# Five matmul passes for six in fc1, by weights in units of their first group's scale, and w2 rounded by ScalarE

## What is computed

```python
# layer 1, on n = layernorm(x)
pre = n @ W + b                                  # 256 x 1024
i, f, o, z = split(pre)
i = 10 * tanh((i + input_bias) / 10);  f = -softplus(f);  o = sigmoid(o);  z = tanh(z)
# a scan over time, for each of the 256 channels, with running maximum m
m' = max(f + m, i);  c = exp(f + m - m') * c + exp(i - m') * z
n' = exp(f + m - m') * n + exp(i - m');  h = o * c / (n' + 1e-6)
x = x + h / rms(h) * scale
# layer 2, on g = layernorm(layernorm(x)) * gamma + beta
w1 = (fc1_q - 128) * fc1_scales[row // 128]      # 256 x 1024, two groups of 128 rows
w2 = (fc2_q - 128) * fc2_scales[row // 128]      # 1024 x 256, eight groups
out = x + 0.5 * (silu(g @ w1 + b1) @ w2 + b2)
```

## Time and profile before

| | |
|---|---|
| median of 3 runs | 316.35 us (316.30 to 316.56) |
| the profiled execution | 317.67 us, its span 315.9 us |
| PE busy | 307.7 us |
| DVE busy | 268.2 us |
| ACT busy | 229.2 us |
| POOL busy | 134.0 us |
| DMA | 16.31 MB |

### The profile page before, as it was taken

The page is one execution under the profiler, slowest core; times in us unless marked ns, Lnnn a source line. Parts: engine busy times, 40 slices in busy tenths (PEclk is TensorE's granted clock), DMA queues, the critical chain, the costliest instruction groups (busy, mean ns, idle before and its releaser), DMA issues.

```text
span 315.9 us, 4861 instructions
## 1 busy us (share of the span) xinstructions
PE 307.7 (97%) x1780; PEld 267.0 (85%) x1780; DVE 268.2 (85%) x473; ACT 229.2 (73%) x372; POOL 134.0 (42%) x131
## 2 busy tenths in 40 slices
PE   8999998998999999999999999999999999999996
PEld 6778787886997889988898889988899899899896
DVE  3999969999999999999989997889969998764431
ACT  3598986698699956798776969489684966931930
POOL 2072177300396258214940188012999365153000
PEclk9999999899999999999999999999999999999999
DMA  7990042410000020021000300000000100100101
GB/s 269 362 381 22 0 83 53 100 33 0 2 1 2 33 100 4 0 76 59 1 2 33 100 2 0 33 32 4 3 0 2 66 0 2 66 0 19 50 2 66
DMA packets 11239, 16.31 MB, mean 52 GB/s; under 512 B 720, under 2 KB 10192, under 8 KB 10704
## 3 DMA queue, kind: packets, MB, share of 16 engines
q1 hardware_dynamic: 10512, 13.12, 12.0%
q0 software_dynamic: 288, 2.10, 3.3%
q10 hardware_dynamic: 416, 0.79, 0.7%
HBM read 9.71 MB, written 4.19 MB: 44 GB/s over the span
## 4 chain that ended last, share of the span: by engine, by line
PE 52%; DVE 26%; POOL 10%; ACT 7%; issue 3%; DMA 1%; DVEq 0%; POOLq 0%; ACTq 0%
PE mm_ps L224 8%; PE mm_ps L226 8%; PE mm_ps L225 8%; PE z_ps L226 6%; PE z_ps L225 6%; PE z_ps L224 6%; POOL rows L1120 3%; DVE y_lo L823 3%; DVE rec L725 3%; DVE rec L732 3%; POOL g L1105 2%; DVE g L791 2%; DVE bn L804 2%; PE t_ps L374 2%; DVE rows L799 2%
## 5 line engine op out<-in xcount | busy, mean ns | idle before, releaser
L224 PE MATMUL z_ps<-w_hi,y_hi 128*128 128x256 f32 x248 | 70.5, 284 | 0.0
L226 PE MATMUL z_ps<-w_hi,y_lo 128*128 128x256 f32 x248 | 69.9, 282 | 0.0
L225 PE MATMUL z_ps<-w_lo,y_hi 128*128 128x256 f32 x248 | 69.9, 282 | 0.0
L551 ACT ACTIVATE y<-mm_ps,b_all 128x512 f32<-128x512 f32 x60 | 41.2, 687 | 13.1 <-PE mm_ps L318 11.1
L823 DVE TENSOR_TENSOR y_lo<-y,y_hi 128x512 fp32r<-128x512 f32 x64 | 42.8, 685 | 8.3 <-ACT y_hi L554 8.1
L225 PEld LDWEIGHTS z_ps<-w_lo,y_hi 128*128 128x128 f32 x248 | 46.8, 189 | 0.3
L224 PEld LDWEIGHTS z_ps<-w_hi,y_hi 128*128 128x128 f32 x248 | 46.6, 188 | 0.4
L226 PEld LDWEIGHTS z_ps<-w_hi,y_lo 128*128 128x128 f32 x248 | 46.7, 188 | 0.0
L224 PE MATMUL mm_ps<-gt_hi,w_hi 128*128 128x512 f32 x108 | 43.4, 401 | 0.0
L226 PE MATMUL mm_ps<-gt_hi,w_lo 128*128 128x512 f32 x108 | 42.8, 396 | 0.0
L225 PE MATMUL mm_ps<-gt_lo,w_hi 128*128 128x512 f32 x108 | 42.7, 396 | 0.0
(11 more groups left out here) (167 smaller groups left out, 687.0 us busy)
## 6 DMA issues: line engine op xcount, KB each, us to landing
out<-rows SPq DMA_DIRECT2D x15, 256.0 KB, 2.1
rows<-x SPq DMA_DIRECT2D x7, 512.0 KB, 6.6
q<-fc_q SPq DMA_DIRECT2D x2, 1024.0 KB, 12.2
w_lo<-q POOLq DMA_DIRECT2D x2, 1024.0 KB, 7.3
s<-fc_scales SPq DMA_DIRECT2D x1, 1024.0 KB, 11.5
wg_raw<-fc_scales SPq DMA_DIRECT2D x1, 1024.0 KB, 11.1
wg_raw<-w_gates SPq DMA_DIRECT2D x1, 512.0 KB, 5.5
wg_raw<-w_gates ACTq DMA_DIRECT2D x1, 512.0 KB, 6.0
```

The costliest lines, as they stand in the source:

```text
L224: pe.matmul(dst, wh[w_at], ah[a_at], start=start, stop=False)
L225: pe.matmul(dst, wh[w_at], al[a_at], start=False, stop=False)
L226: return pe.matmul(dst, wl[w_at], ah[a_at], start=False, stop=stop)
L551: act.activation(y[:, j % YBUFS], fc1_bank(c, j), ACT.Silu, bias=b1_all[:, j:j + 1]).then_inc(silu_done, 1)
```

## The change

Weights of fc1 are held in units of the first group's scale. With u = scale of group 0 for a column, w1 / u is the integer `q - 128` for the first 128 rows, which the rounded format holds exactly, so its low part is dropped and `w1_lo` shrinks to the second 128 rows, which are `(q - 128) * ratio` with ratio = scale 1 / scale 0. `fc1` so takes five passes a tile, and ACT's silu multiplies by `unit` again. For scales near zero, `unit` is the scale plus `tiny`, and `share` (1 - tiny / unit) scales the integers.

The scales now come as one small array, a column per block of 128 features (128 x 16 floats, 8 KB), loaded on ACT's queue as its third load; the broadcast load is gone. POOL makes `tiny` and `unit` ahead of `ln1_root(0)`, DVE 1/unit and `ratio` ahead of `x_normalised(0)`, POOL `share` behind `ln1_root(0)`. PE spreads `ratio` and `share` over the partitions with 8 transposes each, `ratio` into `z_ps` ahead of chunk 0's transposes, `share` into `mm_ps` in the place of the 4 idle passes; ACT copies `share` to SBUF. DVE scales w1 in two operations, block 1 with `z_ps` as an operand, block 0 straight into `w1_hi`, and its rounding of block 0 goes. The order is changed around chunk 0's second norm: `ln1_sums(4)`, `ln1_means(4)` and `ln1_root(4)` are moved ahead, `x_low(3)` comes before w2's scaling, `x_low(2)` before `o_times_c(0)`, ACT's `x_high(2)` before `gates(1, F_TILES)`. w2 is rounded by ACT in two halves, each ahead of a tile of `gates(3)`, instead of by POOL.

```diff
-            sp.dma_start(s1[:], fc1_scales.partition_broadcast(P)).then_inc(s1_in, 16)
...
@@ PE, gates(c, tiles)
-                    if c == 1 and j in Z_TILES:
-                        pass
+                    if c == 0 and j in (2, 3):
+                        pe.wait_ge(share_out, j - 1)
+                    elif c == 1 and j in Z_TILES:
+                        pe.wait_ge(w1_scaled, 1)
@@ PE, fc1(c, tiles)
-                    if j > 0:
-                        for k in range(KD):
-                            ins = three_passes(dst, (w1_hi, w1_lo), (slice(None), k, f), (gt_hi, gt_lo),
-                                               (slice(None), k), k == 0, k == KD - 1)
-                        ins.then_inc(fc1_done, 1)
-                        continue
                     for k in range(KD):
-                        pe.wait_ge(gt_hi_done, at(c, 2, k + 1))
-                        if c == 0 and k == 0:
-                            pe.wait_ge(w1_ready, 16)
+                        if j == 0:
+                            pe.wait_ge(gt_hi_done, at(c, 2, k + 1))
                         pe.matmul(dst, w1_hi[:, k, f], gt_hi[:, k], start=(k == 0), stop=False)
-                        pe.matmul(dst, w1_lo[:, k, f], gt_hi[:, k], start=False, stop=False)
+                    if c == 0 and j == 0:
+                        pe.wait_ge(w1_ready, 16)
+                    pe.matmul(dst, w1_lo[:, f], gt_hi[:, 1], start=False, stop=False)
                     for k in range(KD):
-                        pe.wait_ge(gt_lo_done, at(c, 2, k + 1))
+                        if j == 0:
+                            pe.wait_ge(gt_lo_done, at(c, 2, k + 1))
                         ins = pe.matmul(dst, w1_hi[:, k, f], gt_lo[:, k], start=False, stop=(k == KD - 1))
@@ PE, start
+            def spread(of, bank):
+                for j in range(KF):
+                    ins = pe.transpose(bank(j // 4)[:, j % 4 * P:j % 4 * P + P], of[:, j:j + 1].to_broadcast([P, P]),
+                                       ident[:])
+                return ins
...
             idle_passes(IDLE_PASSES)
             pe.wait_ge(ident_ready, 2)
+            pe.wait_ge(ratio_step, 2)
+            spread(ratio, z_bank).then_inc(ratio_spread, 1)
...
-            idle_passes(IDLE_PASSES // 4)
+            pe.wait_ge(share_ready, 1)
+            spread(share, lambda u: mm_ps[:, 2 + u]).then_inc(share_spread, 1)
@@ ACT, silu and silu_alone
-                    act.activation(y[:, j % YBUFS], fc1_bank(c, j), ACT.Silu, bias=b1_all[:, j:j + 1]
-                                   ).then_inc(silu_done, 1)
+                    act.activation(y[:, j % YBUFS], fc1_bank(c, j), ACT.Silu, bias=b1_all[:, j:j + 1],
+                                   scale=unit[:, j:j + 1]).then_inc(silu_done, 1)
@@ ACT, start and order
             act.dma_start(wg_raw[:, 1], w_gates[P:2 * P, :]).then_inc(wg_in[1], 16)
+            act.dma_start(s1[:], fc1_scale_cols).then_inc(s1_in, 16)
...
             x_high(0)
+            act.wait_ge(share_spread, 1)
+            for u in range(2):
+                act.activation(share_bc[:, u * T:(u + 1) * T], mm_ps[:, 2 + u], ACT.Copy).then_inc(share_out, 1)
...
-            gates(1, F_TILES)
             x_high(2)
-            gates(1, range(4, GJ))
+            gates(1, range(2, GJ))
...
             g_high(0)
-            gates(3, I_TILES)
+            act.wait_ge(w2_scaled, 1)
+            for u in range(2):
+                half = slice(u * KF // 2, (u + 1) * KF // 2)
+                act.activation(w2_hi[:, half], w2_f[:, half], ACT.Copy).then_inc(w2_rounded, 1)
+                gates(3, I_TILES[u:u + 1])
@@ DVE, start and order
             ln1(0)
+            dve.wait_ge(unit_step, 3)
+            dve.reciprocal(per_unit[:], unit[:]).then_inc(ratio_step, 1)
+            dve.wait_ge(ratio_step, 1)
+            dve.tensor_tensor(ratio[:], s1[:, 1], per_unit[:], ALU.mult).then_inc(ratio_step, 1)
             x_normalised(0)
...
-            dve.wait_ge(s1_in, 16)
-            dve.scalar_tensor_tensor(out=w1_f, in0=q1[:], scalar=-ZERO_POINT, in1=s1[:],
+            dve.wait_ge(ratio_spread, 1)
+            dve.scalar_tensor_tensor(out=w1_f, in0=q1[:, 1], scalar=-ZERO_POINT,
+                                     in1=z_ps[:].rearrange("p u n d -> p (u n d)"),
+                                     op0=ALU.add, op1=ALU.mult).then_inc(w1_scaled, 1)
+            dve.wait_ge(share_out, 2)
+            dve.scalar_tensor_tensor(out=w1_hi[:, 0], in0=q1[:, 0], scalar=-ZERO_POINT, in1=share_bc[:],
                                      op0=ALU.add, op1=ALU.mult).then_inc(w1_scaled, 1)
             maximum(0, range(KD))
             x_low(1)
-            dve.wait_ge(w1_scaled, 1)
-            dve.tensor_copy(w1_hi[:, 0], w1_f[:, 0]).then_inc(w1_rounded, 1)
...
             refined(0)
+            x_low(2)
             o_times_c(0)
-            x_low(2)
             h(0)
 
             ln1(3)
             mean_square(0)
+            ln1_sums(4)
...
             ln2(0)
+            ln1_means(4)
+            x_low(3)
...
-            x_low(3)
             maximum(1, range(KD))
             dve.wait_ge(beta_w1, 1)
-            dve.tensor_tensor(b1_all[:], z_ps[:, 0, 0, 0:KF], col[:, COL_B1:COL_B1 + KF], ALU.add
-                              ).then_inc(b1_ready, 1)
+            dve.tensor_tensor(b1_all[:], z_ps[:, 0, 0, 0:KF], unit[:], ALU.mult).then_inc(b1_ready, 1)
+            dve.wait_ge(b1_ready, 1)
+            dve.tensor_tensor(b1_all[:], b1_all[:], col[:, COL_B1:COL_B1 + KF], ALU.add).then_inc(b1_ready, 1)
...
             mean_square(1)
-            ln1_sums(4)
...
             ln2(1)
-            ln1_means(4)
@@ POOL
+            pool.wait_ge(s1_in, 16)
+            pool.tensor_tensor(tiny[:], s1[:, 0], s1[:, 0], ALU.mult).then_inc(unit_step, 1)
+            pool.wait_ge(unit_step, 1)
+            pool.tensor_scalar(tiny[:], tiny[:], TINY * TINY, 2.0 * TINY, ALU.is_lt, ALU.mult).then_inc(unit_step, 1)
+            pool.wait_ge(unit_step, 2)
+            pool.tensor_tensor(unit[:], s1[:, 0], tiny[:], ALU.add).then_inc(unit_step, 1)
             pool.wait_ge(half_ready, 1)
             ln1_root(0)
+            pool.wait_ge(ratio_step, 1)
+            pool.tensor_tensor(share[:], tiny[:], per_unit[:], ALU.mult).then_inc(unit_step, 1)
+            pool.wait_ge(unit_step, 4)
+            pool.tensor_scalar(share[:], share[:], -1.0, 1.0, ALU.mult, ALU.add).then_inc(share_ready, 1)
...
-            negated(w1_lo, w1_hi, w1_negated)
+            negated(w1_lo[:], w1_hi[:, 1], w1_negated)
...
             ln2_root(0)
-            pool.wait_ge(w2_scaled, 1)
-            pool.tensor_copy(w2_hi[:], w2_f).then_inc(w2_rounded, 1)
-            pool.wait_ge(w2_rounded, 1)
-            pool.wait_ge(gt_hi_done, at(0, 2, 1))
+            ln1_root(4)
+            pool.wait_ge(w2_rounded, 2)
...
             ln2_root(1)
-            ln1_root(4)
```

More of the change, by code:

```diff
@@ L32 @@
 YBUFS = 4
+TINY = 2.0 ** -60
 IDLE_PASSES = 16
@@ L43, in exists, with layer @@
     return 0 <= c < CHUNKS
-def layer(nc, x, w_gates, cols, scale_row, fc1_q, fc1_scales, fc2_q, fc2_scales, b2_row, out):
+def layer(nc, x, w_gates, cols, scale_row, fc1_q, fc1_scale_cols, fc2_q, fc2_scales, b2_row, out):
     x_view = x.rearrange("s (c t p) d -> s c p t d", t=TT, p=P)
@@ L62, in layer @@
         w1_hi = sb("w1_hi", [P, KD, F], F32R)
-        w1_lo = sb("w1_lo", [P, KD, F], F32R)
+        w1_lo = sb("w1_lo", [P, F], F32R)
         w2_hi = sb("w2_hi", [P, KF, D], F32R)
@@ L69, in layer @@
         q2 = sb("q2", [P, KF, D], I32)
-        s1 = sb("s1", [P, KD, F])
+        s1 = sb("s1", [P, KD, KF])
+        tiny = sb("tiny", [P, KF])
+        unit = sb("unit", [P, KF])
+        per_unit = sb("per_unit", [P, KF])
+        ratio = sb("ratio", [P, KF])
+        share = sb("share", [P, KF])
+        share_bc = sb("share_bc", [P, F])
         s2 = wg_raw[:].rearrange("p k (h d) -> p (k h) d", d=D)
-        w1_f = q1[:].bitcast(F32)
+        w1_f = q1[:, 1].bitcast(F32)
         w2_f = q2[:].bitcast(F32)
@@ L157, in layer @@
         w1_scaled, w1_rounded, w1_ready = sem("w1_scaled"), sem("w1_rounded"), sem("w1_ready")
+        unit_step, ratio_step, share_ready = sem("unit_step"), sem("ratio_step"), sem("share_ready")
+        ratio_spread, share_spread, share_out = sem("ratio_spread"), sem("share_spread"), sem("share_out")
         w2_scaled, w2_rounded, w2_ready = (sem(n) for n in ("w2_scaled", "w2_rounded", "w2_ready"))
@@ L288, in fc1 @@
                     if c == 0 and j in (4, 5):
-                        pe.wait_ge(b1_ready, 1)
+                        pe.wait_ge(b1_ready, 2)
                     elif c == 0 and j >= 6:
@@ L391, in shifted_bias @@
             def shifted_bias():
-                pe.wait_ge(w1_scaled, 1)
+                pe.wait_ge(w1_scaled, KD)
                 pe.wait_ge(gate_done, at(1, 8, 6))
@@ L395, in shifted_bias @@
                     for k in range(KD):
```

(14 more changed lines are left out.)

8 lines of the change are left out of this document (4 added, 4 removed).

## The result

The changed kernel takes **313.59 us** (median of 4 runs, 313.36 to 313.88) against 316.38 (4 runs, 316.30 to 316.56): a ratio of 0.9903, 95% interval 0.9887 to 0.9919. That is 2.8 us of gain where 6.25 were forecast. The profiled execution took 313.88, with a span of 311.9 us.

A forecast was written before the change was run, and what follows sets the result against it. PE was busiest, but joins with DVE, POOL and ACT would pass on only part of its 15.0 us: -4.2 at `g_turned(6)`, -0.45 and -1.6 in the tail make -6.25, so 310.1 us from the median 316.35, range 305 to 314.8.

The forecast's parts named there:

- POOL's chain: From `ln2(5)` to `g_turned(6)`, 219 to 259 us: no fc1 pass in it; moves by 2.95, `base(4)` gives 1.25, so -4.2.
- all four joins: PE would wait at `h_turned(2)`, `h_turned(4)`, `g_turned(6)` (about 2 us) and `g_turned(7)` (about 1.4).
- (a): PE sets the end throughout, DVE and POOL follow: 303.5 us; chance 0.12.
- (b): The chunk's period is DVE's and POOL's own, only the tail's 2.05 shows: 314.9 us; chance 0.10.
- Rival (c): PE's clock falls at the start, in a gap behind the idle passes: costs 1.7 us, 311.8 us; chance 0.12.
- (d): `s1` lands late, at 14.3 us, the start is +8.9 and the kernel gets slower: 318.4 us; chance 0.06.
- the sum at `divisor(1)`: Chunk 0's second norm: 2.0 + 0.6 + 0.45 + 0.25 - 1.7 - 1.5 + 1.0 = +1.1 us.
- the scan of `denominators(1)` that took 2.78 loses 1.5: DVE in chunk 0's second norm: the scan ran beside a POOL operation of 2048 columns; 1.5 us booked as gain.
- ACT's 1.25 us a tile: ACT's silu and copy back to back, against 1.17 for PE's five passes, so ACT sets the pace of `fc1`.
- the tail: After `g_turned(6)`: 0.45 us won before `g_turned(7)`, then 1.6 of the 1.87 us saved in `fc1(7)`.
- The contention: POOL's negation of w2 runs beside a later stretch of DVE: costs 0 to 1.5 us, 1.0 taken.
- The start: Chunk 0 waits for `s1`, landing at 7.6 us, and small operations: `x_normalised(0)` at 9.9 instead of 7.64, +2.2.

The follow-up runs named there:

- the run of the five passes alone: The kernel before with one of fc1's six passes a tile left out and nothing else of the change: 309.97 us (ratio 0.9796).
- The repeat: The kernel before, unchanged, run and profiled once more: 316.24 us (12 runs), span 314.5 us.
- the three other profiles named with it: The kernel before with one fc1 pass dropped (309.97 us), with silu scales from a tile of ones (315.21), and with 32 unused bytes (314.94).
- a kernel with another start: The changed kernel with s1 loaded one place earlier and the scale steps behind chunk 0's first norm: 310.97 us; without the silus' operand 309.47.
- the pieces: The changed kernel with POOL's negation of w2 in four instructions of 512 columns instead of one of 2048: 312.37 us (ratio 0.987).
- the five other profiles: The changed kernel without silu operand (311.41 us), with w2's negation in four (312.37), 64 unused bytes (313.20), a sixth pass (317.55), the old order (314.21).

## Why the prediction was wrong in size

**The mechanism was right.** Most of the 15 us taken off PE never reaches the end; nothing is won by 102 us; POOL's chain and ACT's silus hold the rest. PE waited at all four joins, was busy for 295.4 us (forecast near 293), and `base(4)` lost 1.09 of its 5.13 us (1.25 taken), though POOL's root beside it grew from 1.00 to 1.97. Rivals (a) and (b) fall with the run of the five passes alone, 309.97. Rival (c) did not happen: the first gates ran at the granted clock 1.00. Of (d) only a landing by 8.3 us happened.

**The step that failed first** is in the sum at `divisor(1)`: "the scan of `denominators(1)` that took 2.78 loses 1.5". That length was a chance of the one execution profiled, the greater part of the very 1.3 us by which it exceeded the median. I took it as a gain of the change and then set the whole -6.25 against the median, which doesn't have it. Without this term the sum is -4.75, and 311.6 us. The repeat and the three other profiles named with it show the scan at 1.27.

**Two more terms were mis-sized.** The silus' scale: I took "ACT's 1.25 us a tile" from the earlier trace rows for a silu without that operand; it was 1.33 to 1.35. This is 1.5 us at the end by the runs, 0 in my sum, and in the tail alone 0.8 where I had 1.6. The Trainium skill ("ScalarE: Activation LUTs", section "What ACT_TABLE_LOAD costs") gives some 93 ns for each per-partition pointer operand; the trace agrees with its 0.09, and I had not looked the operand up. The contention: 1.46 us of DVE, where I took 1.0 out of bounds of 0 to 1.5. The two are 2.0, which leaves 2.8 of the 4.75, and 2.8 were measured. That this fits so well is in part luck: the operand's 1.5 comes from a kernel with another start, and the gains of the pieces and of the start did not add.

**The start is open.** In the profile it cost +2.8 for the +2.2 of the sum, with the scales at 8.3 us, not 7.6. In the five other profiles it was as forecast (9.59 to 9.82 for 9.9), or 2.2 to 2.4 later than in the repeat of the kernel before. If the timed executions of the changed kernel started late, 2.15 of the 4.75 are left, and 0.6 came back by what no run sorted out; that the moved tiles let PE's passes follow each other faster may be part of it.

## What to carry to other kernels

Before a long instance of an instruction is booked as a gain, see whether a second execution has it too, and profile the changed kernel twice as well: a sum made on one execution may only be set against the median once the difference between the two is located. Cost each new operand and each small load at the head of a serial start, because most of a us lost there reaches the end (2.6 us of time for 2.99 at the first norm), while work taken off the busiest engine reaches it only as far as the engine behind it lets it. Where several engines nearly tie, give work to the one that waits in that stretch, as DVE did in chunk 7.

## What the hardware did that I had not expected

- **One of the two at a time.** DVE and POOL did not slow each other; one stood still until the other's instruction ended. A copy of 4 elements took 1.63 us (0.17 alone) and a sum of 8 columns 1.90, each ending with POOL's operation; POOL's took 1.90 undisturbed and 2.63 to 2.86 when it came behind. A difference of 0.5 us in who is first turned a wait of 1.5 us in one scan of DVE into 0.3 in the next scan and 0.8 in POOL's operation. The Trainium skill ("Trainium Architecture — The Big Picture", section "What this means for kernel authors") calls the pair's shared port an exclusive lock and not a split of bandwidth, and these rows agree.
- **32 unused bytes** in front of the tiles shorten the distance between PE's passes of 256 columns from 120.0 to 117.0 ns and the kernel from 316.4 to 314.9 us. In the changed kernel 64 took it from 119.2 to 117.2. So a change that declares a tile can move PE's pace by that alone; a run with only the declaration tells the two apart.
- **8 KB** took 6.5 us to land behind 768 KB on its queue at the start (5.6 to 5.8 in the five other profiles), and 5.1 and 4.6 behind 256 KB, in two profiles with an issue 0.5 us earlier.
- **The granted clock fell without idle time.** From 49 to 54 us, with the one-column passes of `shifted_bias`, PE was busy all 5.00 us in the changed kernel, and from 54 to 58 the granted clock was 0.63; in the kernel before PE had been idle for 1.1 us there, and it was 0.58. What both had were the one-column passes, so the idle time of rival (c) need not have been the cause.
